# fp16 halves and crossbar transposes in a fused attention and FFN kernel

## What is computed

```python
xn = layernorm(x)
# attention, 16 heads of 16, window of 128 keys ahead of the query
q, k = l2norm(xn @ Wq.T), l2norm(xn @ Wk.T);  v = xn @ Wv.T
a = softmax(q @ k.T + alibi_and_mask) @ v
s = a @ Wo.T
# FFN, every operand rounded to FP4 in blocks of 16 (scale = max|block| / 6)
h = silu(fp4(xn) @ fp4(w_gate).T) * (fp4(xn) @ fp4(w_up).T)      # 704 wide
out = x + s * silu(fp4(h) @ fp4(w_down).T)
```

## Time and profile before

| | |
|---|---|
| median of 3 runs | 508.33 us (507.36 to 508.8) |
| span of the profiled execution | 507.1 us |
| what lies around it, against the median | 1.2 us |
| PE busy | 471.6 us, 93% of the span |
| DVE, POOL, ACT busy | 85%, 82%, 79% |
| mean granted TensorE clock | 0.983 of full speed |

### The profile page before, as it was taken

The page is one execution under the profiler, slowest core; times in us unless marked ns, Lnnn a source line. Parts: engine busy times, 40 slices in busy tenths (PEclk is TensorE's granted clock), DMA queues, the critical chain, the costliest instruction groups (busy, mean ns, idle before and its releaser), DMA issues.

```text
span 507.1 us, 14045 instructions
## 1 busy us (share of the span) xinstructions
PE 471.6 (93%) x4990; PEld 409.0 (81%) x4990; DVE 429.2 (85%) x865; ACT 402.6 (79%) x584; POOL 415.7 (82%) x929
## 2 busy tenths in 40 slices
PE   0367989999999999999999999999999999999997
PEld 0356768888888888888989888888898888888886
DVE  4989988889888888888989888888898888887685
ACT  1456988988888888888887888888888888888952
POOL 6554679899989989899997898989999899888651
PEclk9967999999999999999999999999999999999999
DMA  8211011222322113222222222222222221122100
GB/s 303 81 43 43 13 29 45 64 74 75 74 59 48 51 36 65 64 63 64 65 64 45 62 34 53 63 55 53 53 54 54 52 46 29 37 53 53 44 22 32
DMA packets 78276, 29.35 MB, mean 58 GB/s; under 512 B 67712, under 2 KB 77696, under 8 KB 78208
## 3 DMA queue, kind: packets, MB, share of 16 engines
q1 hardware_dynamic: 77920, 28.39, 22.2%
q10 hardware_dynamic: 288, 0.08, 0.1%
HBM read 7.49 MB, written 4.19 MB: 23 GB/s over the span
## 4 chain that ended last, share of the span: by engine, by line
PE 82%; DVE 1%; ACT 1%; issue 1%; POOL 1%; DVEq 0%; POOLq 0%
PE gt L348 12%; PE up L348 11%; PE bank_b L592 11%; PE gt L545 11%; PE bank_q L348 8%; PE bank_b L354 6%; PE gt L354 6%; PE scores L499 5%; PE gt L567 5%; PE bank_b L348 4%; PE gt L549 1%; PE up L499 1%; PE scores L348 0%; PE up L567 0%; ACT pv_t L1196 0%
## 5 line engine op out<-in xcount | busy, mean ns | idle before, releaser
L1318 ACT ACTIVATE probs<-scores 128x1024 f32<-128x1024 f32 (+1 forms) x101 | 102.5, 1015 | 3.4 <-PE scores L499 2.1
L1503 POOL TENSOR_SCALAR_AFFINE_SELECT probs<-probs 128x512 f32<-128x512 f32 x128 | 81.4, 638 | 3.0 <-ACT probs L1318 2.7
L1510 POOL TENSOR_SCALAR_AFFINE_SELECT probs<-probs 128x512 f32<-128x512 f32 x120 | 75.9, 634 | 3.7
L592 PE MATMUL bank_b<-probs,vals 128*32 128x128 f32 x1952 | 59.7, 274 | 0.4 <-DVE vals L928 0.3
L592 PEld LDWEIGHTS bank_b<-probs,vals 128*32 128x32 f32 x1952 | 51.4, 110 | 7.0 <-DVE vals L928 6.1
L1196 ACT ACTIVATE qk_stack<-bank_q 128x512 f16<-128x512 f32 x64 | 35.2, 597 | 21.8 <-DVE bank_q L907 21.8
L781 DVE TENSOR_TENSOR xT_lo<-gt,xT_hi 128x512 fp32r<-128x512 f32 (+1 forms) x34 | 22.3, 657 | 31.1 <-ACT xT_hi L1196 31.1
L545 PE MATMUL gt<-wdn_hi,hT_hi 128*128 128x256 f32 x160 | 47.8, 299 | 0.6 <-DVE hT_lo L833 0.6
L545 PE MATMUL gt<-wdn_hi,hT_lo 128*128 128x256 f32 x160 | 45.1, 282 | 0.0
L545 PE MATMUL gt<-wdn_lo,hT_hi 128*128 128x256 f32 x160 | 45.0, 281 | 0.0
L348 PE MATMUL up<-wgu_hi,xT_hi 128*128 128x352 f32 x124 | 43.2, 349 | 0.3 <-DVE h_grid L822 0.3
(11 more groups left out here) (219 smaller groups left out, 1650.9 us busy)
## 6 DMA issues: line engine op xcount, KB each, us to landing
out<-y SPq DMA_DIRECT2D x32, 128.0 KB, 2.0
x_all<-x SPq DMA_DIRECT2D x20, 128.0 KB, 2.0
x_all<-x SPq DMA_DIRECT2D x3, 512.0 KB, 4.0
x_all<-wproj SPq DMA_DIRECT2D x1, 768.0 KB, 6.7
dn_raw<-wd SPq DMA_DIRECT2D x1, 704.0 KB, 8.3
probs<-wg SPq DMA_DIRECT2D x1, 640.0 KB, 5.3
probs<-wu SPq DMA_DIRECT2D x1, 640.0 KB, 7.2
qk_slots<-qk_stack SPq DMA_TRANSPOSE x32, 3.7
```

The lines of the kernel that those rows point to most:

```text
L592: done = e.matmul(pv_bank(i)[32 * n:32 * n + 32, grp * P:(grp + 1) * P], va, pr, start=part == 0, stop=part == 1 or final(i))
L1318: e.activation(probs[j % P_BUFS][:, grp, :, side(j), :], score_banks(j, grp)[:, :, :, side(j), :].rearrange("p b e h q -> p (b e) h q"), A ...
L1503: e.affine_select(out=own, in_=own, compare_op=ALU.is_ge, fill=0.0, base=0, pattern=[[0, GRP], [-1, P]], channel_multiplier=1).then_inc(s_ ...
L1510: e.affine_select(out=part, in_=part, compare_op=ALU.is_gt, fill=0.0, base=0, pattern=[[0, GRP], [1, P]], channel_multiplier=-1).then_inc( ...
```

## The change

All wide products go to fp16. The weights wproj, wo, wgu and wdn, and the transposed x, h and attention rows are stored as two fp16 tiles, hi and lo, and a product keeps its three terms. fp16 has a narrow range, so weights and h are scaled by powers of two, which ACT, PE and DVE work out at the start (sums of absolute values, `sum_*`, `tr_bound`, `powers`, `steps`), and which later operations take back out through a scalar operand.

x, h and attention rows are no longer transposed on PE. ACT writes their hi half and DVE their lo half, both in fp16 and side by side in a stack in SBUF, and SP issues a crossbar DMA for each stack and turn: 8 blocks for x, 15 for attention and h together. q_h's first, 64 wide part is gone. The down and output products of a tile come one turn later, behind scores group 3. x and h chains count each step on a semaphore of its own. The orders of all five engines are new; on POOL each step of the root is placed by itself, with a mask and q_x in between.

```diff
-        wgu = [sb(f"wgu_{p}", [P, KT, 2 * FF], F32R) for p in ("hi", "lo")]
+        wgu = [sb(f"wgu_{p}", [P, KT, 2 * FF], F16) for p in ("hi", "lo")]
...
+        x_ring = sb("x_ring", [P, XN_BUFS + 2, D])
+        xn = [x_ring[:, i] for i in range(XN_BUFS)]
+        xq = [x_ring[:, XN_BUFS + i] for i in range(2)]
+        x_stack = [sb(f"x_stack{i}", [P, 2, 2, D], F16) for i in range(2)]
...
+        ah_all = sb("ah", [P, 2, D + FF])
+        ah_stack = [sb(f"ah_stack{i}", [P, AH_SLOTS * P], F16) for i in range(2)]
+        ahT = [sb(f"ahT{i}", [P, AH_SLOTS, P], F16) for i in range(2)]
...
             def lo_x(u):
                 e.wait_ge(s_hi_x, u + 1)
-                hi, lo = (flat(z[:, turn_parts(u), :]) for z in xT[u % 2])
-                e.tensor_tensor(lo, bank_c[:, turn_cols(u)], hi.bitcast(F32), ALU.subtract).then_inc(s_lo_x, 1)
+                hi, lo = (x_stack[u % 2][:, turn_parts(u), p, :] for p in range(2))
+                e.tensor_tensor(lo, turn_rows(u), hi, ALU.subtract).then_inc(s_lo_x, 1)
...
+            def lo_ah(g):
+                e.wait_ge(s_hi_ah, g + 1)
+                hi = ah_stack[g % 2][:, 0:TAIL_BOTH * P]
+                e.tensor_tensor(ah_stack[g % 2][:, ATT_LO * P:], ah_all[:, g % 2, 0:TAIL_BOTH * P], hi,
+                                ALU.subtract).then_inc(s_lo_ah, 1)
...
             def hi_x(u):
-                e.wait_ge(s_tr_x, u + 1)
...
+                copy(x_stack[u % 2][:, turn_parts(u), 0, :], turn_rows(u)).then_inc(s_hi_x, 1)
+            def hi_ah(g):
+                e.wait_ge(s_att, g + 1)
+                e.wait_ge(s_q_h, g + 1)
...
+                copy(ah_stack[g % 2][:, 0:D + FF], ah_all[:, g % 2, :]).then_inc(s_hi_ah, 1)
...
-                e.tensor_tensor(blocks(h_q[t % 2][:, FF:FP]), blocks(h_grid[:, FF - TAIL:FF]),
-                                per_block(h_scale[:, (FF - TAIL) // QB:]), ALU.mult)
...
-                e.tensor_scalar(z, tmp, -10.0 / 3.0, None, ALU.add).then_inc(s_rs, 1)
+                    e.tensor_scalar(z, tmp, 1.0, -10.0 / 3.0, ALU.mult, ALU.add).then_inc(s_rs, 1)
...
+            def x_transpose(u):
+                e.wait_ge(s_lo_x, u + 1)
...
+            def ah_transpose(g):
+                e.wait_ge(s_lo_ah, g + 1)
+                e.wait_ge(s_lo_tail, g + 1)
...
+                e.dma_start_transpose(ahT[g % 2][:], ah_stack[g % 2][:]).then_inc(l_ahT[g % 2], 16)
```

The weight sums at the start, the first of five:

```diff
+            def sum_gu():
+                e.wait_ge(l_wg, 32)
+                e.wait_ge(l_wu, 32)
+                e.activation(junk[:, 0:n_gu], gu_raw, ACT.Abs, accum_out=sums[:, 0:1]).then_inc(s_sum_gu, 1)
```

More of the change, by code:

```diff
@@ L1038, in vector_program @@
-            up_x(0)
             norm_w(4)
-            lo_x(1)
-            grid_x(0)
+            powers(1)
             round_w(4)
             squares(1)
+            lo_x(2)
+            norm_x(1)
+            root(1)
             values(0)
-            root(1)
-            wide_x(1)
-            ln_moments(4)
-            rscale_x(1)
-            unit(1)
-            values(1)
-            norm_x(1)
-            scales_w(WD_SCALES)
+            unit(1)
+            scales_w(WD_SCALES)
+            lo_qk(1)
@@ L1068, in vector_program @@
-            norm_x(2)
-            ln_moments(5)
             amax_h(0)
             unit(2)
+            lo_x(3)
             wide_h(0)
+            ln_stats(5)
             rscale_h(0)
-            lo_x(3)
+            ln_moments(5)
+            lo_qk(2)
+            rscale_x(2)
             norm_h(0)
-            lo_qk(2)
+            amax_x(3)
+            norm_x(2)
+            ln_stats(6)
+            up_h(0)
+            wide_x(3)
+            squares(3)
             up_x(2)
+            grid_h(0)
@@ L1107, in vector_program @@
             attend(0)
+            up_h(1)
             norm_x(4)
[L1109 to L1125 removed]
+            squares(4)
+            grid_h(1)
+            lo_tail(0)
+            values(4)
+            up_x(4)
+            ln_stats(7)
+            lo_ah(0)
+            lo_x(5)
+            grid_x(4)
+            ln_moments(7)
+            amax_x(5)
+            wide_x(5)
+            rscale_x(5)
+            ln_stats(8)
+            for t in range(4, 31):
+                norm_x(t + 1)
                 unit(t)
+                if exists(t + 2):
+                    amax_x(t + 2)
                 hidden(t - 2)
[L1128 removed]
                 lo_qk(t)
@@ L1185, in vector_program @@
             attend(TILES - 1)
[L1186 to L1187 removed]
+            up_h(TILES - 1)
+            lo_tail(TILES - 2)
+            grid_h(TILES - 1)
+            lo_ah(TILES - 2)
+            q_h_last()
             lo_tail(TILES - 1)
+            lo_ah(TILES - 1)
+            gated(TILES - 3)
             gated(TILES - 2)
@@ L1610, in gpsimd_program @@
+            root(-1, ROOT)
             x_norm(0)
+            x_norm(1)
             norm_w(1)
             scale_x(0)
+            pad_stack(0)
+            steps(0)
+            ln_parts(2)
+            norm_w(3)
+            ones(0)
             round_w(1)
-            norm_w(3)
             floor_ss(0)
-            x_norm(1)
-            ln_parts(2)
+            norm_w(5)
+            pad_stack(1)
+            q_x(0)
+            ones(1)
+            scale_x(1)
             x_norm(2)
+            ln_parts(3)
@@ L1619, in gpsimd_program @@
             round_w(3)
-            q_x(0)
-            norm_w(5)
-            ones(1)
-            ones(2)
-            scale_x(1)
-            ones(3)
-            ln_parts(3)
             floor_ss(1)
             x_norm(3)
+            round_w(5)
+            steps(1)
+            ln_parts(4)
+            ones(2)
+            mask_own(0, 2)
+            floor_ss(2)
+            root(2, SEED)
+            root(2, Y_SQ)
+            root(2, ARG)
+            root(2, LINEAR)
+            q_x(1)
@@ new lines, in gpsimd_program @@
+            x_norm(4)
+            scale_h(0)
+            ln_parts(5)
+            mask_prev(1, 2)
+            mask_prev(1, 3)
+            floor_ss(3)
+            root(3, SEED)
+            ones(3)
+            root(3, Y_SQ)
+            root(3, ARG)
+            q_x(2)
+            root(3, LINEAR)
+            root(3, QUAD)
+            scale_x(3)
+            mask_own(1, 0)
+            root(3, CUBIC)
+            root(3, STEP)
+            root(3, Z_SQ)
+            root(3, Z_ARG)
+            mask_prev(2, 0)
```

1178 lines of the change are left out of this document (626 added, 552 removed).

## The result

The changed kernel takes 542.55 us (median of 4 runs, 540.99 to 543.96), against 508.02 us for the kernel before in the same comparison: a ratio of 1.068, 95% interval 1.0656 to 1.0707. The forecast was 524 us in a range of 498 to 540. The sign was right; the loss is more than twice the forecast's, and the time lies above the range.

A forecast was written before the change was run, and what follows sets the result against it. POOL was taken to bound the kernel at 14.12 us a turn. With 14.45 after, the loop adds 8.9 us, the start 3.5 and the end 3.5 to 508.3: 524.2 us, range 498 to 540.

The forecast's parts named there:

- Ahead of the loop: Before turn 4: weight sums on ACT (4.8 us) and a later first product add 3.5 us, between 0 and 7.
- What bounds the kernel before: In the steady loop, POOL is full from end to end and its ledger is the 14.12 us turn.
- the turn of tile 16: Loop turn where POOL skips four masks; its 13.83 us was read as what the other engines allow, about 13.8.
- POOL's own terms: POOL's list in the loop: 0.60 us a turn removed, from 14.12 to 13.52, before the exclusion is charged.
- the exclusion: In the loop, DVE operations with two SBUF inputs hold up POOL: 1.21 us a turn gross, net 0.94.
- The two-operation form: Two additions in POOL's root take 0.23 instead of 0.32 us each, 0.17 a turn for both.
- up to three gaps of 0.09 absorb part: 0.27: POOL's idle gaps between root steps swallow 0.27 us a turn of the exclusion's 1.21, leaving 0.94.
- Late transposes: Rival: in the loop, attention and h transposes land late, down products start 1 to 2 us late; about 550 us; chance 0.06.
- Exclusion paid in idle time: Faster rival: POOL waits for DVE in the loop, which hides the charge; 501 us, 494 to 506; chance 0.26.
- DVE's own waits: Rival: DVE's six two-input operations wait for POOL, 0.5 us a turn more; 537 us; chance 0.10, shared with upper end.
- Behind the loop: After the loop: last h by DMA +2.6 us, its copy and lo about +0.9; +3.5 in all, between 0 and 6.
- level: Behind the loop, one more down product and twelve fewer transposes for each of three turns cancel out.

The follow-up runs named there:

- run 5: Kernel before with the two additions in POOL's root in two-operation form, nothing moved; 507.3 us, ratio 0.998.
- run 12: Kernel before with the split products in fp16 halves and nothing else of the change; 501.6 us, ratio 0.9878.
- run 1: Kernel after, but in the loop the lo of x, attention and h, and tail take their second input from PSUM instead of SBUF; 510.8 us, ratio 1.0056.
- Runs 1 to 3: Run 1; then the same with lo of x unchanged, 516.5 us; then kernel before with three lo operations reading first inputs from SBUF, 528.1 us.
- run 9: Kernel after with the lo of x 3 and x 4 ahead of the scaling of q and k of tiles 2 and 3; 539.3 us, ratio 1.0622.
- run 8: Kernel after with each of the three weight sums at the start on 64 columns only; 540.3 us, ratio 1.0638.
- run 7: Kernel after with x 0's transpose ahead of a wait on SP, lo_tail(29) earlier, last h scaled ahead of lo_ah(30); 545.3 us, ratio 1.0719.

## Why the prediction was wrong

The mechanism in the loop was right, and its sum 4.4 us short (13.3 against 8.9). Ahead of the loop 8.6 us were missing and behind it 3.2, so three quarters of the error lie at the ends.

- **What bounds the kernel before.** "POOL is thus full from end to end; I take 14.12 us as its ledger": true as a sum, wrong as a cause, or at least not the cause alone. Taking 0.18 us from POOL moved nothing (run 5), relieving TensorE moved the turn to 14.00 (run 12). The text had PE's 14.07 of 14.10 and passed over it. It didn't spoil the sum, since the change takes TensorE down to 12.1 us a turn. Nor do the others allow 13.8, as read from the turn of tile 16: that tile spares TensorE products too, and with TensorE relieved the other turns of run 12 stay at 14.00.
- **POOL's own terms.** Without the exclusion the prediction had 13.52 a turn; run 1 measured 13.48. The two-operation form gives 0.09 a step, as said, where nothing collides; beside lo_ah it hides behind the collision (312 against 224 ns).
- **The exclusion.** Its gross price, 1.21 us, is what the turn shows (14.69 against 13.48), and some of that is luck: lo_x was put at 0.41 and costs 0.31, lo_ah with the tail was put at 0.80 and costs 0.90. The step that failed is the next one, "up to three gaps of 0.09 absorb part: 0.27". Nothing was absorbed: the gaps between dependent steps stay (idle of 0.09 before each, about 2.0 us in 24 turns, in runs and kernel alike), and POOL idles 1.13 us a turn in the kernel after and 1.14 in run 1. That is 0.24 us a turn, 6.5 over 27, less 2 by which the last two turns are short. The Trainium skill says that a VectorE instruction with two SBUF inputs contends with a GpSimd instruction that reads SBUF (SBUF — State Buffer, Who interferes with whom). Runs 1 to 3 agree: taking these inputs away gives 1.21 us a turn back (14.69 to 13.48), and three added ones in the kernel before cost 0.70 (14.12 to 14.82).
- **Rivals.** Late transposes: PE waits 0.6 us a turn for ahT in the kernel after, a sign that the prediction would have taken for an error; it costs nothing in the loop, since POOL is later. Ahead of the loop (run 9) and at the end transposes do cost. Exclusion paid in idle time: excluded by run 1. DVE's own waits: lo_ah is held up about 0.2 us a turn, but DVE still waits 1.9 us for POOL's root, so they don't set the turn.
- **Ahead of the loop**, +3.5 foreseen (end of the range 7), +12.1 measured: the largest error. The sums were priced right (4.6 us) and were nearly worthless (run 8). The step that failed is that the sums and the first product's delay stand for the loop's, with DVE's longer list put at nothing. The first product itself came 9.4 us later, and 4.8 of these were worth nothing (run 7). Tile 0 is scaled 9.35 us later at the end of DVE's list, in which DVE is busy 24.7 us where it was 16.8; the other 2.7 us come by turn 4, where run 9 wins back 3.3 and loses 1.5 of it in the next turn. Part of the busy time is collision again, also in operations with one input. DVE's timeline of the kernel after:

```profile
8.32 1.74 DVE L946 TENSOR_SCALAR probs<-probs 128x64 f32<-128x64 f32 x1
...
12.99 0.23 DVE L946 TENSOR_SCALAR probs<-probs 128x64 f32<-128x64 f32 x1
...
30.34 1.05 DVE L820 TENSOR_SCALAR rsq<-ss 128x33 int32<-128x33 int32 x1 [0.27 <-POOL ss L1575]
```

  and POOL's beside the first:

```profile
8.21 1.80 POOL L1480 MEMSET vals<- 128x2048 f32 x1
```

  The same operation takes 0.23 or 1.74 us; the long one ends with POOL's memset. The prediction counted two-input operations alone. The Trainium skill says that a tensor_scalar can enter a 2-port mode, and that whoever comes second then blocks fully (SBUF — State Buffer, Who interferes with whom). The row fits it: the memset began at 8.21, DVE's operation at 8.32, and both end at 10.0 to 10.1. In DVE's list up to the scaling of tile 0, six operations, of one input and of two, take 4.8 us more in all than their like undisturbed, an estimate from the timeline; how much of the 9.35 us they cause, no run separates, and the cause of that delay stays open in part.
- **Behind the loop**, +3.5 foreseen (end 6), +6.7 measured. From the last h scaled to its down product the way is 7.2 us (526.16 to 533.39) against 2.7 before (497.58 to 500.24): +4.6 where 3.5 was foreseen. The last three ah transposes land 4.2 to 4.9 us after their stacks are done, the last at 4.9; the prediction had 3.7. The rest isn't "level": from the scaling in turn 31 to the last h the stretch is 31.0 us, before 27.8. DVE waits 3.5 us there for PE's up product, but before it waited as long for ACT's copy of transposed h, so why the stretch is longer stays open. After the last landing it is 1.0 us shorter.

The profile after should have shown PE at 12.5 us a turn (12.1), root steps 0.4 to 0.9 longer (0.84, 0.27 and 0.20), L907 every 14.45 us (14.69), DVE waiting about 1 us for the root (1.9), the first q,k product 3 us later (9.4).

## What to carry to other kernels

Before an operand moves from PSUM to SBUF, count DVE's operations that then have two SBUF inputs and charge each to GpSimd's list, no gap deducted: here about 0.3 us for 512 columns and 0.9 for 896 and a tail of 64. When several engines look full over a stretch, read that stretch's window for each and relieve one at a time: in the kernel before, TensorE's dtype alone gave 1.2%, while 0.18 us a turn taken off POOL, the engine with the long chain, left the turn as it was. And in a prologue price what stands in the busiest engine's list ahead of the last hand-over, not the first thing that is late.
